# Latent attention: 4 key tiles turned on TensorE and 12 through DRAM, two maxima ahead of the 32x32 transposes, side products in PSUM banks of their own, head products in DRAM

## What is computed

```python
h = layernorm(x)
c_q, c_kv = h @ w_down_q.T, h @ w_down_kv.T          # 128 -> 64 each
q, k, v = (up-projections of c_q, c_kv, c_kv)        # 16 heads of 64
q, k = rope(q), rope(k)
scores = einsum('bhqd,bhkd->bhqk', q, k) * scale
out = softmax(scores) @ v
out = out @ w_out.T + residual
```

## Time and profile before

| | |
|---|---|
| time, median of 3 runs | 2226.29 us (2221.23 to 2229.69) |
| the profiled execution | 2230.09 us |
| its span, first to last instruction | 2228.3 us |
| TensorE busy | 1976.1 us, 89% |
| VectorE busy | 1563.6 us, 70% |
| ScalarE busy | 1330.9 us, 60% |
| GpSimd busy | 1078.9 us, 48% |
| moved by DMA | 374.20 MB |

### The profile page before, as it was taken

One profiled execution on the slowest core, in us unless ns is written; L12 is line 12 of the kernel. 1 busy time (PEld: TensorE's weight loads), 2 busy tenths in 40 slices (PEclk: granted clock), 3 DMA queues, 4 the chain that ended last, 5 costly groups with the idle time before them and its releaser, 6 DMA issues. The chain is left out here.

```text
span 2228.3 us, 37533 instructions
## 1 busy us (share of the span) xinstructions
PE 1976.1 (89%) x11974; PEld 990.4 (44%) x11974; DVE 1563.6 (70%) x2431; ACT 1330.9 (60%) x2587; POOL 1078.9 (48%) x1225
## 2 busy tenths in 40 slices
PE   5847898889668999999999999999999999995596
PEld 2543585458433444443444444444444444442254
DVE  6787665966656777777777776777776777772644
ACT  5524683667205777776777776777776777772121
POOL 0726641843034665664665654665654665653000
PEclk8978899989868999999999999999999999997698
DMA  1001300030054777676777676687676787673000
GB/s 35 1 1 64 74 3 29 6 75 4 11 195 150 272 263 257 248 285 228 255 277 261 239 279 238 245 285 261 239 269 237 246 285 261 239 268 110 0 1 19
DMA packets 195075, 374.20 MB, mean 168 GB/s; under 512 B 11888, under 2 KB 156912, under 8 KB 193840
## 3 DMA queue, kind: packets, MB, share of 16 engines
q1 hardware_dynamic: 194864, 371.61, 47.5%
HBM read 182.82 MB, written 171.44 MB: 159 GB/s over the span
## 5 line engine op out<-in xcount | busy, mean ns | idle before, releaser
L1585 DVE TENSOR_REDUCE g.lowest<-g_score 128x1 f32<-128x1024 f32 x514 | 619.6, 1206 | 331.0 <-PE g_score L1553 331.0
L1599 ACT ACTIVATE g.probs<-g_score,g.lowest 128x1024 f32<-128x1024 f32 x514 | 573.4, 1116 | 322.5 <-DVE g.lowest L1585 322.5
L1553 PE MATMUL g_score<-g.keys,g.queries 64*128 64x512 f32 x2056 | 514.9, 616 | 21.9 <-issue 11.1
L1685 DVE STREAM_TRANSPOSE g.blocks<-g.probs 128x640 f32<-128x640 f32 x513 | 426.2, 831 | 0.9
L1615 PE MATMUL g_mix_ps<-g.far,mid.y_tok 128*64 128x512 f32 x1320 | 323.7, 604 | 0.0
L1553 PEld LDWEIGHTS g_score<-g.keys,g.queries 64*128 64x128 f32 x2056 | 174.1, 187 | 275.3 <-ACT g.probs L1599 156.4
L1574 PEld LDWEIGHTS g_work<-top.ident,g.probs 128*128 128x128 f32 x1536 | 164.5, 141 | 195.6 <-ACT g.near L1578 94.0
L1574 PE MATMUL g_work<-top.ident,g.probs 128*128 128x128 f32 x1536 | 225.3, 283 | 0.0
L1578 ACT ACTIVATE g.near<-g_work 128x768 f32<-128x768 f32 x256 | 205.5, 803 | 10.7 <-PE g_mix_ps L1615 10.6
L1705 POOL TENSOR_TENSOR mid.y_tok<-mid.y_tok,g.waves 128x512 f32<-128x512 f32 x128 | 162.6, 1270 | 101.3 <-ACT mid.y_tok L1568 101.3
L1615 PE MATMUL g_mix_ps<-g.near,mid.y_tok 128*64 128x512 f32 x792 | 199.9, 612 | 0.7 <-ACT g.mixed L1623 0.7
(11 more groups left out here) (364 smaller groups left out, 2898.1 us busy)
## 6 DMA issues: line engine op xcount, KB each, us to landing
g.far<-bounce SPq DMA_DIRECT2D x257, 640.0 KB, 5.7
bounce<-g.blocks SPq DMA_DIRECT2D x256, 640.0 KB, 5.7
g.far<-g.near SPq DMA_DIRECT2D x7, 640.0 KB, 5.7
lt0.v_late<-la0.v SPq DMA_DIRECT2D x6, 512.0 KB, 9.6
lt1.v_late<-la1.v SPq DMA_DIRECT2D x6, 512.0 KB, 9.9
bounce<-g.near SPq DMA_DIRECT2D x4, 640.0 KB, 6.9
top.upto<-g.mixers SPq DMA_DIRECT2D x33, 64.0 KB, 5.7
lt.turns<-turns SPq DMA_DIRECT2D x1, 2048.0 KB, 8.2
```

The lines of the kernel that those rows point to most:

```text
L1553: nc.tensor.matmul(score[:, 2 * pair + odd], queries[rows, turn, head, cols], keys[rows, turn, head, pair * CH:(pair + 1) * CH], start=Tru ...
L1585: nc.vector.tensor_reduce(lowest[:, unit, half, r:r + 1], score[:, 2 * half:2 * half + 2].rearrange("p b n -> p (b n)"), AX.X, ALU.max, ne ...
L1599: nc.scalar.activation(probs[:, r % 2, half * 2 * CH:(half + 1) * 2 * CH], score[:, 2 * half:2 * half + 2].rearrange("p b n -> p (b n)"), ...
L1685: nc.vector.transpose(blocks[:, r, :, REST * half:REST * (half + 1)].rearrange("p j t c -> p t j c"), probs[:, r % 2, at:at + REST * P].re ...
```

## The change

- `NEAR` goes from 6 to 4: TensorE turns 4 tiles of 128x128 per step and the copy into `near` has 512 elements per partition; VectorE's two transposes per step have 768 elements for 640, and each write and read through DRAM 768 KB for 640.
- The PSUM tile `work` becomes `turned` (one bank, which all four tiles fill) and `side` (two banks). The waits that the shared bank needed go: TensorE waits for a side copy just ahead of the side product that overwrites it, and ScalarE has both exponentials ahead of the copy in every step.
- VectorE takes both maxima of the next row block, then both transposes of this one. `blocks_turned` counts once per step, and an exponential waits for the transposes of two steps before.
- The second head product is taken in step 4 instead of 6, its copy on ScalarE in step 5 instead of 7, and GpSimd has its `add_output` ahead of `totals` and `coefs`.
- `mixers` shares its space with `blocks`; the head products are stored to DRAM once (18 x 64 KB, ahead of the dummies on SP's queue) and each is loaded from there.

```diff
-NEAR = 6
+NEAR = 4
...
-        mixers = sp.sb("mixers", [P, 2 + HEADS_G, D])
+        blocks = sp.sb("blocks", [P, RT, 4, FAR, 32])
+        mixers = blocks[:, 0:2].rearrange("p r j t c -> p (r j t c)")[:, 0:(2 + HEADS_G) * D].rearrange("p (h n) -> p h n", n=D)
+        stored_mixers = nc.dram_tensor("stored_mixers", (2 + HEADS_G, P, D), F32).ap()
...
-        work = sp.ps("work", [P, 3, CH])
-        turned, side = work[:, 0:2], work[:, 1:3]
+        turned = sp.ps("turned", [P, CH])
+        side = sp.ps("side", [P, 2, CH])
...
         def load_mixer(sync, kind, slot):
-            sync.dma_start(mixer_now[kind][:], mixers[:, bass.ds(slot, 1)].rearrange("p a n -> p (a n)"))\
+            sync.dma_start(mixer_now[kind][:], stored_mixers[bass.ds(slot, 1), :, :].rearrange("a p n -> (a p) n"))\
                 .then_inc(mixer_loaded[kind], 16)
...
                 load_w(sync, 1, 1)
+                sync.dma_start(stored_mixers.rearrange("h p n -> p h n"), mixers).then_inc(m["mixers_stored"], 16)
...
+                sync.wait_ge(m["mixers_stored"], 16)
                 load_mixer(sync, 0, 1)
...
             if free:
-                act.wait_ge(m["blocks_turned"], 2 * G + half - 1)
+                act.wait_ge(m["blocks_turned"], G + 1)
...
-        def turn_blocks(dve, r, half, G):
-
-            dve.wait_ge(m["exp_done"], 2 * G + half + 1)
-            if half == 0:
-                dve.wait_ge(written[r], 4 * (G - r) + 16)
-            at = half * 2 * CH + TURN * P
-            nc.vector.transpose(blocks[:, r, :, REST * half:REST * (half + 1)].rearrange("p j t c -> p t j c"),
-                                probs[:, r % 2, at:at + REST * P].rearrange("p (t j a) -> p t j a", j=4, a=32))\
-                .then_inc(m["blocks_turned"], 1)
+        def turn_blocks(dve, r, G):
+
+            dve.wait_ge(m["exp_done"], 2 * G + 2)
+            dve.wait_ge(written[r], 4 * (G - r) + 16)
+            for half in range(2):
+                at = half * 2 * CH + TURN * P
+                ins = nc.vector.transpose(blocks[:, r, :, REST * half:REST * (half + 1)].rearrange("p j t c -> p t j c"),
+                                          probs[:, r % 2, at:at + REST * P].rearrange("p (t j a) -> p t j a", j=4, a=32))
+            ins.then_inc(m["blocks_turned"], 1)
...
         def write_blocks(sync, w, r, G):
-            sync.wait_ge(m["blocks_turned"], 2 * G + 4)
+            sync.wait_ge(m["blocks_turned"], G + 3)
...
                             make_parts(pool, 1 - turn, 2 * j + 1, H + 1, 1)
+                            add_output(pool, (2 * j + 2) % 4, (j + 3) % NC, H + 1)
                             totals(pool, this, H)
                             coefs(pool, this, H)
-                            add_output(pool, (2 * j + 2) % 4, (j + 3) % NC, H + 1)
...
                                     pe.wait_ge(m["near_copied"], G + 1)
-                                    if step == 1:
-                                        pe.wait_ge(m["out_taken"], H + 2)
-                                    elif step == 2:
-                                        pe.wait_ge(m["piece_taken"], H + 1)
-                                    elif step == 4:
-                                        pe.wait_ge(m["piece_taken"], H + 2)
-                                    elif step == 7:
-                                        pe.wait_ge(m["out_taken"], H + 3)
                                     turn_tiles(pe, r)
...
-                                    if step in (0, 1, 3, 6):
-                                        pe.wait_ge(m["near_copied"], G + 2)
...
                                     elif step == 1:
+                                        pe.wait_ge(m["out_taken"], H + 2)
...
                                     elif step == 3:
+                                        pe.wait_ge(m["piece_taken"], H + 1)
                                         pieces(pe, 1 - turn, 2 * j + 1)
-                                    elif step == 6:
+                                    elif step == 4:
+                                        pe.wait_ge(m["piece_taken"], H + 2)
...
-                                    row_max(dve, unit, (r + 1) % RT, 0, G + 1)
-                                    turn_blocks(dve, r, 1, G)
-                                    row_max(dve, unit, (r + 1) % RT, 1, G + 1)
+                                    for half in range(2):
+                                        row_max(dve, unit, (r + 1) % RT, half, G + 1)
...
-                                    turn_blocks(dve, (r + 1) % RT, 0, G + 1)
+                                    turn_blocks(dve, r, G)
...
+                                    elif step == 5:
+                                        take_output(act, H + 1)
                                     elif step == 6:
                                         falls(act, H)
                                     elif step == 7:
-                                        take_output(act, H + 1)
                                         take_mixed(act, U + 1)
...
                                     exps(act, unit, (r + 1) % RT, 0, G + 1)
-                                    side_next = step in (0, 1, 3, 6)
-                                    if not side_next:
-                                        exps(act, unit, (r + 1) % RT, 1, G + 1)
+                                    exps(act, unit, (r + 1) % RT, 1, G + 1)
...
                                     copy_tiles(act, w, r)
-                                    if side_next:
-                                        exps(act, unit, (r + 1) % RT, 1, G + 1)
```

More of the change, by code:

```diff
@@ L1414, in latent_attention @@
         far = sp.sb("far", [P, 2, RT * 4, FAR, 32])
-        blocks = sp.sb("blocks", [P, RT, 4, FAR, 32])
         lowest = sp.sb("lowest", [P, 4, 2, RT])
@@ L1573, in turn_tiles @@
                     at = half * 2 * CH + k * P
-                    ins = nc.tensor.transpose(turned[:, half, k * P:(k + 1) * P], probs[:, r % 2, at:at + P], ident[:])
+                    to = (TURN * half + k) * P
+                    ins = nc.tensor.transpose(turned[:, to:to + P], probs[:, r % 2, at:at + P], ident[:])
             ins.then_inc(m["turn_done"], 1)
         def copy_tiles(act, w, r):
-            nc.scalar.activation(near[:, w, :, r * P:(r + 1) * P].rearrange("p (k t) n -> p k t n", k=2),
-                                 turned[:, :, 0:TURN * P].rearrange("p k (t n) -> p k t n", n=P), ACT.Copy)\
+            nc.scalar.activation(near[:, w, :, r * P:(r + 1) * P], turned[:].rearrange("p (t n) -> p t n", n=P), ACT.Copy)\
                 .then_inc(m["near_copied"], 1)
@@ L1842, in _ @@
                 pe.wait_ge(m["mixed_ready"], UNITS + 1)
-                pe.wait_ge(m["near_copied"], 4 * UNITS + 1)
-                output(pe, mixers[:, HEADS_G + 1])
+                pe.wait_ge(mixer_loaded[0], 16 * (UNITS // 2 + 1))
+                output(pe, mixer_now[0])
                 pe.wait_ge(landed[0], 64 * (4 * PAIRS_G + 1))
```

7 lines of the change are left out of this document (3 added, 4 removed).

## The result

The changed kernel takes 2157.07 us (median of 4 runs, 2151.45 to 2158.43), the kernel before 2227.99 in the same comparison. The ratio is 0.9681 [0.9666, 0.9695]: 3.2% faster. The forecast was 2148 us, 3.5% faster, with a range of 2130 to 2190.

A forecast was written before the change was run, and what follows sets the result against it. TensorE's stream was taken to bound the loop: 2230.09 (profiled execution) - 79.7 (loop) + 1.5 (tail) = 2151.9 us; that execution being 3.8 above the median, the forecast was 2148 us, range 2130 to 2190.

The forecast's parts named there:

- TensorE's stream sets the loop: Loop of 256 steps: TensorE's back-to-back work sets 97% of it; short-step floor falls from 4.49 to 4.28 us.
- The new period 38.43: Eight-step period: new floor 38.18 us plus 0.25 for waits, against 40.92 measured before; gain 2.49 us x 32.
- 1.06 us are stalls: Period before the change: 40.92 us measured less a floor of 39.86, spread over steps 0, 3, 5 and 6.
- I leave 0.25 us: Allowance per new period for waits that the addition of the dependence chain does not see.
- two causes: Second exponential's delay: VectorE's transpose between the maxima, and ScalarE's copy ahead of it in steps 0, 1, 3, 6.
- the stalls stay as they are, 53.8: Lower bound of the loop's gain: only the transposes' 1.68 us per period is won, x 32 = 53.8 us.
- The ring of the new order: Scores through maxima and exponentials to the next scores: 3.96 us, 0.32 under the 4.28 step, so no stall.
- the rival that makes it the pace: VectorE paces the short steps, 4.48 us each; gain only 48 us, 2180 us; chance 0.2.
- The rival by occupancy: VectorE, busy 77% of the loop, is the pace; 68 to 77 us slower, 2296 us; chance 0.02.
- DMA, cost 0 in the loop: Writes and reads grow to 768 KB, 331 GB/s needed; queues had moved 394 to 420, so no loop time lost.
- Tail +1.5: After the loop: later last write and longer transfers cost 0 to 3.0 us; the middle taken.
- the 2151.9 of the sum: Forecast for the profiled execution: 2230.09 less 79.7 in the loop plus 1.5 in the tail.

The follow-up runs named there:

- near4_shared: Kernel before with four tiles and DRAM head products only; shared bank, transpose between maxima and old orders stay: 2200.75 us, 0.9863.
- pad_dve: Changed kernel with one more VectorE instruction per step, a memset of 256 elements behind the transposes: 2157.43 us, 0.9684.
- mix_first: Changed kernel with the quarter of a mix ahead of the four transposes of the same step on TensorE: 2148.86 us, 0.9649.
- near2: Changed kernel with two tiles turned by TensorE and fourteen over DRAM, mix quarters moved by one: 2257.35 us, 1.0147 against the kernel before.
- half_reads: Changed kernel with half of each block's read from DRAM left out, save the last ones: 2148.79 us, 0.9648.

## Why the prediction was right

- *TensorE's stream sets the loop*: right, and by its starts, not by its busy time. The floor of a step came at 4.27 for 4.28, transposes to mix at 0.58 for 0.59, two transposes at 0.22 for 0.21.
- *The new period 38.43*: measured 38.49. The two halves of the term were mis-sized against each other. "1.06 us are stalls" was wrong: 0.40 of them are the 4 x 0.10 of scores that are not behind a side product, and stay. "I leave 0.25 us" for waits was too much: there are none. The errors are 0.40 and 0.25 and 0.08 on the transposes, and cancel to 0.06, or 2 us in all.
- *Why the stalls go*: half right. The prediction named two causes and let both count. VectorE's transpose between the maxima is the one that matters: 0.41 of 0.66 us before, and 1.45 us once the tiles are four. The side product's wait for the copy was 0.25 us with six tiles, and with four nothing that can be measured. What the prediction also missed is that the bound "the stalls stay as they are, 53.8" was no bound for four tiles in the old order: with a transpose in it the ring is 4.71 us, longer than the new short step, and near4_shared gained 30 us. The ring of the new order was 0.07 too long, 3.96 for 3.89, and well under the step either way.
- *VectorE*: right, its work a little less (4.10 for 4.18, and 4.37 in a step with floors), and the rival that makes it the pace is out by pad_dve. The rival by occupancy is out as well. By the rule of the Trainium skill (Perfetto Trace Analysis, Identifying the Most-Contended Engine) VectorE was the contended engine, at 77% against 43% for TensorE's weight loads; adding to VectorE and taking from TensorE made the kernel 3.2% faster, so here the trace does not agree with it. The section asks for MFU beside the weight loads, and that was not worked out here, so only this half of its rule is answered.
- *GpSimd*: right, 2.8 us left for 2.9.
- *DMA, cost 0 in the loop*: right for the steps, wrong for the margin. "The queues moved 394 GB/s over 5 us and 400 to 420 in the set-up" was no measure of what this mix of writes and reads can hold, which is 353. The new kernel uses 325 to 333 of it.
- *The 17.4 us of the passes of the hardware loop, left as they are*: 16.4 in the profile. They vary by some us from one execution to another, with the idle time and the clock at each wrap, and the prediction had no term for that.
- *Tail +1.5*: measured +4.3, outside its bounds of 0 to 3. The last mix does wait for its data; the reads take 1.3 us longer in the median than before, not 0.3, and 1.25 us go to the lower clock behind the wait, for which the prediction had no term.
- *Set-up hidden*: right. The profile of the changed kernel has its first maximum at 676.1 us, that of before at 680.4; the 4.3 us lie in the unchanged layers ahead, and in the second execution of the same kernel it is at 679.2. So it is luck that the profiled execution (2151.45) met the 2151.9 of the sum: +2.8 for the tail and +1.0 for the loop stand against -4.3 ahead of it. Against the medians, 70.9 us are gained and not 78.6, and the forecast of 2148 is 9 too low. Of these, 3.8 are the tail and the loop and 1.7 that the kernel before stood 2.1 above its median of four and not 3.8; the rest no trace shows, since in both comparisons the profiled execution of the changed kernel was its fastest.

The fastest kernel that does all the work is mix_first at 2148.86 us. Its interval touches that of the changed kernel, so it is at most a little better. To go further, a period would have to lose TensorE's work without putting more through DRAM.

## What to carry to other kernels

Write the time of a loop as two numbers: the stream of the bounding engine, and the ring of dependences through the others; the longer one is the step, and an edit that shortens one is worth only what the other allows (30 and 9 us apart, 70 together here). Before you call a difference a stall, look whether it stands in the same places at the same size in every period. A time that repeats to 0.01 us in every step can still vary by some us at the wraps of a loop, so compare steps before you give a difference of medians a cause. Take the ceiling of the DMA from a kernel that is bound by it with the same mix of transfers, not from a burst.

## What the runs showed of the hardware that was not expected

- Scores of 64 rows take 1.92 us behind a mix or transposes of 128 rows and 1.82 behind another product of 64 rows, in all the timelines shown here. In the first case the load of the first weights starts with the product (1412.80), in the second 0.11 us ahead of it (1408.42 for 1408.53). Side products behind a mix load theirs in the open as well (1407.53 for 1407.54). The cause is open.
- The DMA holds 351 to 353 GB/s at 98 to 99% busy with writes to DRAM and reads from it mixed, while in slices of about one us in the set-up it moved 400 to 420. The Trainium skill (DMA: Bandwidth & Descriptors, Measured) has 425 GB/s for one core reading 16 MB at a time; no run here came near that for long. At the first wrap of the changed kernel, with the other engines all but idle, it moved 402 GB/s for 3.7 us, so 353 is not all that the queues can do; what holds it there is not shown.
- A wait of TensorE can cost more than itself. Behind the 3.45 us of near2 the granted clock is 0.50 for 3.8 us, 1.2 instead of 2.4 GHz, and the mix of 12 pieces takes 5.32 us to the next product, where the same at full clock takes 2.72 (1408.02 to 1410.74). It does not always: behind the 3.96 us at the first wrap of the changed kernel the clock stays at 1.00 (to 996.10), behind the 3.78 at the second it falls to 0.50, and the scores there take 3.42 us to the transposes (1304.44 to 1307.86) for 1.92.
- A wrap of the hardware loop leaves TensorE idle for 3.4 to 4.0 us in the changed kernel and in the one before, and for 1.8 to 2.1 at two of three wraps of half_reads and of mix_first. The kernels with the lower DMA load are on both sides.
